# A matrix-memory attention layer between two routed FFNs: output steps moved by chunks, norm double-buffered, biases folded

## What is computed

```
xn = LN(x) * g + b ;  x_t = xn W_up_l + b ;  r_t = xn W_up_r + b
x_c = silu(causal_conv(x_t))                    # conv along features
q, k = x_c W_q + b, (x_c W_k + b) / 8 ;  v = x_t W_v + b ;  o = sigmoid(x_t W_o + b)
i, f = 15 tanh((x_c W + b) / 15)                # per head
m_t = max(f + m, i); c = exp(f - m_t + m) c + exp(i - m_t) v k^T ; n likewise
h   = o * (c q) / max(n q, 1)                   # 8 heads of 64, scan over 512 tokens
hn  = LN_head(h) * mh_g + mh_b
out = (hn + x_c W_skip + b) * silu(r_t) ; result = out W_down + b + x
```

## Time and profile before

| | us |
|---|---|
| runs of the kernel before (3) | 540.03, 540.77, 541.8; median 540.77 |
| profiled execution, whole | 539.02 |
| its span | 537.2 |
| mean granted TensorE clock | 0.885 |
| ffn(0) up to the last block | about 107 |
| attention, its head included | about 107 to 440 |
| ffn(1) | to 537 |

### The profile page before, as it was taken

The page is one execution under the profiler, slowest core; times in us unless marked ns, Lnnn a source line. Parts: engine busy times, 40 slices in busy tenths (PEclk is TensorE's granted clock), DMA queues, the critical chain, the costliest instruction groups (busy, mean ns, idle before and its releaser), DMA issues.

```text
span 537.2 us, 9897 instructions
## 1 busy us (share of the span) xinstructions
PE 392.7 (73%) x3018; PEld 329.4 (61%) x3035; DVE 343.2 (64%) x988; ACT 207.7 (39%) x528; POOL 194.9 (36%) x172
## 2 busy tenths in 40 slices
PE   0851499907998799897999988898998632049990
PEld 0720499904786677675777766676776522049990
DVE  5677277777259787379684497892889425027763
ACT  0230144435444474544635355634554100014440
POOL 5248244430005542224353054223062532724451
PEclk9996599957999999999979998999998755559996
DMA  8999222120000000000000000000004000112215
GB/s 299 296 327 209 54 66 69 59 88 2 0 1 1 2 2 1 1 0 0 0 0 0 0 0 0 0 0 0 1 1 157 2 0 10 49 46 69 68 56 166
DMA packets 26394, 28.23 MB, mean 53 GB/s; under 512 B 2977, under 2 KB 23329, under 8 KB 25857
## 3 DMA queue, kind: packets, MB, share of 16 engines
q1 hardware_dynamic: 22144, 19.13, 13.6%
q0 software_dynamic: 2496, 5.13, 2.9%
q10 hardware_dynamic: 1728, 3.65, 1.9%
HBM read 18.69 MB, written 9.21 MB: 52 GB/s over the span
## 4 chain that ended last, share of the span: by engine, by line
PE 50%; DVE 18%; POOL 9%; DMA 8%; issue 8%; ACT 5%; DVEq 0%; SPq 0%; ACTq 0%; POOLq 0%
PE bank L760 45%; POOL slots L467 6%; DMA slots<-QKT 3%; PE bank L1028 1%; DVE X L1149 1%; DMA X<-x 1%; PE bank L938 1%; DVE XN L1167 1%; PE bank L827 1%; DMA QKT<-by_token 1%; DVE CS L1512 1%; DMA by_token<-YB,IDX 1%; ACT WVT L656 1%; ACT E L665 1%; DMA slots<-XN,POS 1%
## 5 line engine op out<-in xcount | busy, mean ns | idle before, releaser
L493 POOL TENSOR_TENSOR HS<-HS,MHALF 128x8 f32<-128x8 f32 x16 | 26.3, 1644 | 202.6 <-DVE HS L1544 202.6
L473 POOL DMA_INDIRECT by_token<-YB,IDX x46 | 44.5, 968 | 60.1 <-DVE YB L1254 59.5
L760 PE MATMUL bank<-XBT,W1R 128*128 128x128 f32 x368 | 52.8, 290 | 0.0
L656 ACT ACTIVATE WVT<-bank,AC 128x128 f32<-128x128 f32 x128 | 36.5, 374 | 36.5 <-PE bank L760 36.5
L760 PE MATMUL bank<-W,HT 128*128 x368 | 49.2, 278 | 0.0
L467 POOL DMA_INDIRECT slots<-XN,POS x32 | 35.3, 1102 | 38.4 <-DMA slots<-QKT 17.2
L760 PEld LDWEIGHTS bank<-XBT,W1R 128*128 128x128 f32 x368 | 48.0, 204 | 0.6 <-ACT XBT L562 0.2
L827 PE MATMUL bank<-K,XB 128*128 128x128 f32 x46 | 13.6, 296 | 46.0 <-DMA XB<-slots 45.8
L760 PEld LDWEIGHTS bank<-W,HT 128*128 128x128 f32 x368 | 45.5, 195 | 0.3
L562 ACT ACTIVATE XBT<-bank 128x128 f32<-128x128 f32 x46 | 12.8, 277 | 84.5 <-PE bank L827 84.5
L620 ACT ACTIVATE QKT<-bank,COLS 128x512 f32<-128x512 f32 x32 | 22.0, 687 | 38.8 <-PE bank L760 38.8
(11 more groups left out here) (281 smaller groups left out, 1039.7 us busy)
## 6 DMA issues: line engine op xcount, KB each, us to landing
W<-w SPq DMA_DIRECT2D x2, 2048.0 KB, 13.4
slots<-QKT SPq DMA_DIRECT2D x2, 1483.5 KB, 25.3
XB<-slots SPq DMA_DIRECT2D x46, 64.5 KB
W<-w SPq DMA_DIRECT2D x1, 2064.0 KB, 22.9
QKT<-by_token SPq DMA_DIRECT2D x8, 256.0 KB, 4.2
X<-x SPq DMA_DIRECT2D x4, 256.0 KB, 4.9
BROWS<-rowpack SPq DMA_DIRECT2D x1, 1024.0 KB, 12.6
out<-X SPq DMA_DIRECT2D x4, 256.0 KB, 2.3
```

The costliest lines, as they stand in the source:

```text
L473: g.indirect_dma_start(out=by_token[f], out_offset=bass.IndirectOffsetOnAxis(ap=IDX[:, j:j + 1], axis=0), in_=YB[:, j, :], in_offset=None) ...
L493: step.do(g.tensor_tensor(HS[:, 3, :], HS[:, 2, :], MHALF[:, 0:H], ALU.pow))
L656: ins = a.activation(DT[:, hf, m, :], DM[:, m * P:(m + 1) * P], ACT.Exp, bias=AC[:, c, h:h + 1])
L760: return t_.matmul(o, l, r, start=start, stop=stop, skip_group_check=True)
```

## The change

Six things are done.

- VectorE: `centre` is cut into `divide` and `centre`; both for chunk `c` now stand in chunk `c + 1`, with `weigh` between them. `gate` and `transpose_out` of chunk `c` come in chunk `c + 2`, the transpose behind its `values`; `norm_moments` moves from chunk 1 to chunk 0, `silu` and `gate_scans` inside chunk 3.
- The transpose bank's order follows (`TR_USES`).
- `H2` has two buffers, `H2S[c % 2]`; the second lies over `YB`.
- The norm's g and b and the biases of v, o and r are folded into the weights at the start, through a column of ones in place of feature 0 of `ZB`; the v, o and r projections have no bias matmul, the s projection has one of an fp32r row pair. `XT` and one load (`WUL`) go.
- These weights are split during the setup, no longer behind the last block.
- On ScalarE, `out_t` and the head's copies change places accordingly.

```diff
-        TR_USES = ["k0", "k1", "u0", "k2", "u1", "o0", "d0", "k3", "u2", "o1", "d1", "o2", "d2", "o3", "d3"]
+        TR_USES = ["k0", "k1", "u0", "k2", "u1", "k3", "u2", "o0", "d0", "o1", "d1", "o2", "d2", "o3", "d3"]
...
-        H2 = w1r_flat[:, 0:HID].rearrange("p (h d) -> p h d", h=H)
+        H2S = [w1r_flat[:, 0:HID].rearrange("p (h d) -> p h d", h=H),
+               YB[:, :, :].rearrange("p j d -> p (j d)").rearrange("p (h d) -> p h d", h=H)]
...
             def head_in(b):
 
                 act.wait_ge(*pj_full_at(b, "z"))
-                a.activation(XT[:, :], PJ[0][:, :], ACT.Identity, scale=col("g"), bias=col("b"))
-                a.activation(XTH[:, :], PJ[0][:, :], ACT.Identity, scale=col("g"), bias=col("b"))\
-                 .then_inc(pj_free[0], 1)
+                a.activation(XTH[:, :], PJ[0][:, :], ACT.Copy).then_inc(xt_high, 1)
...
                 if c:
                     decays(b, c, 0)
-                if c >= 2:
-                    out_t(b, c - 2)
+                if c == 3:
+                    out_t(b, 0)
                 if last and c == 3:
                     xn_channels(1, 0)
                 if nxt:
                     take(*nxt, "v")
+                if c == 3 and not last:
+                    round_xc(b + 1)
                 decays(b, c, 1)
                 if c:
                     squares(b, c - 1)
...
                     xn_channels(1, 1)
                 if nxt:
                     take(*nxt, "o")
+                if c == 3 and not last:
+                    head_gates(b + 1)
                 state_decays(b, c)
-                if c == NC - 1 and not last:
-                    round_xc(b + 1)
-                    head_gates(b + 1)
                 if nxt:
                     take(*nxt, "r")
                 if c < NC - 1:
...
             def sequence(b, last):
                 for c in range(NC):
                     chunk(b, c, last)
-                if not last:
-                    for m in range(3):
-                        head_qk(b + 1, m)
+                if last:
+                    out_t(b, 1)
+                    squares(b, 3)
+                    out_t(b, 2)
+                    out_t(b, 3)
+                    return
+                head_qk(b + 1, 0)
+                out_t(b, 1)
+                head_qk(b + 1, 1)
                 squares(b, 3)
-                if not last:
-                    head_qk(b + 1, 3)
+                head_qk(b + 1, 2)
+                head_qk(b + 1, 3)
                 out_t(b, 2)
-                if not last:
-                    for m in range(4, 8):
-                        head_qk(b + 1, m)
-                    take(b + 1, 0, "s")
-                    head_columns(b + 1)
-                    decays(b + 1, 0, 0)
+                for m in range(4, 8):
+                    head_qk(b + 1, m)
+                take(b + 1, 0, "s")
+                head_columns(b + 1)
+                decays(b + 1, 0, 0)
                 out_t(b, 3)
...
                 dst = pj_wait(b, f"{what}{c}")
-                mm(dst[:, :], ONES3[:, :], BIAS3[:, i * HID:(i + 1) * HID], True, False)
-                for x_, w_ in parts:
-                    ins = mm3(dst[:, :], x_, w_, False, x_ is parts[-1][0])
+                if what == "s":
+                    mm(dst[:, :], ONESR[:, :], SKIPB[:, :], True, False)
+                for n, (x_, w_) in enumerate(parts):
+                    ins = mm3(dst[:, :], x_, w_, what != "s" and n == 0, n == len(parts) - 1)
...
-                if c >= 2:
-                    transpose_out(b, c - 2)
                 if last and c == 3:
 
                     xn_channels(1, 0)
                 if nxt:
                     project(*nxt, "v")
                 decays(b, c, 1)
-                if c >= 2:
-                    down_out(b, c - 2)
+                if c == 3:
+                    down_out(b, 0)
                 if nxt:
                     project(*nxt, "o")
                 if last and c == 3:
...
                 from_state(b, c)
                 if more:
                     to_state(b, c)
+                if c == 2 and not last:
+                    head_x(b + 1)
                 values(b, c)
+                if c >= 2:
+                    transpose_out(b, c - 2)
                 if last and c == 3:
                     for q in range(3):
                         logits(1, q)
-                if c == 2 and not last:
-                    head_x(b + 1)
 
             def open_sequence(b):
 
...
                 for c in range(NC):
                     chunk(b, c, last)
                 if last:
+                    down_out(b, 1)
                     for c in (2, 3):
                         transpose_out(b, c)
                         down_out(b, c)
                     return
-                head_qk(b + 1, WQH, WQL, "q", lambda: head_carry(b + 1))
+
+                def after_first():
+                    down_out(b, 1)
+                    head_carry(b + 1)
+
+                head_qk(b + 1, WQH, WQL, "q", after_first)
                 transpose_out(b, 2)
                 head_qk(b + 1, WKH, WKL, "k", lambda: down_out(b, 2))
                 project(b + 1, 0, "s")
...
             def low_xt(b):
-                dve.wait_ge(*pj_read_at(b, "z"))
-                v.tensor_tensor(XTL[:, :], XT[:, :], XTH[:, :].bitcast(F32), ALU.subtract).then_inc(xt_low, 1)
+                dve.wait_ge(xt_high, b + 1)
+                v.tensor_tensor(XTL[:, :], PJ[0][:, :], XTH[:, :].bitcast(F32), ALU.subtract).then_inc(pj_free[0], 1)
...
-            def centre(b, c):
+            def divide(b, c):
...
                 dve.wait_ge(hv_read, n + 2)
+            def centre(b, c):
+
+                H2 = H2S[c % 2]
                 dve.wait_ge(*pj_read_at(b, f"o{c}"))
...
             def chunk(b, c, last):
                 more = c < NC - 1
                 if c:
+                    divide(b, c - 1)
                     weigh(b, c, 0)
+                    if c == 3 and not last:
+                        silu(b + 1)
+                    centre(b, c - 1)
+                    if c == 3:
+                        update_x(b, 0)
                 else:
                     take_k(b, 0)
-                if c >= 2:
-                    update_x(b, c - 2)
-                if c:
-                    variance(b, c - 1)
                 if more:
                     take_k(b, c + 1)
                 weigh(b, c, 1)
                 scale_q(b, c)
-                if c == 3 and not last:
-                    low_xc(b + 1)
-                    gate_scans(b + 1)
-                    take_r(b + 1, 0)
                 if more:
                     take_r(b, c + 1)
+                elif not last:
+                    low_xc(b + 1)
+                if c:
+                    variance(b, c - 1)
+                if c == 0 and not last:
+                    norm_moments(b + 1)
+                if c == 1 and not last:
+                    scale_norm(b + 1)
+                if c == 2 and not last:
+                    low_xt(b + 1)
+                if c >= 2:
+                    gate(b, c - 2)
                 if last and c == 0:
                     layer_moments(1, 0)
                 if last and c == 2:
                     layer_norm(1, 0)
-                if c == 1 and not last:
-                    norm_moments(b + 1)
                 if more:
                     new_state(b, c)
-                if c == 2 and not last:
-                    low_xt(b + 1)
-                if c:
-                    gate(b, c - 1)
-                if c == 1 and not last:
-                    scale_norm(b + 1)
-                centre(b, c)
-                if c == 2 and not last:
-                    silu(b + 1)
+                elif not last:
+                    gate_scans(b + 1)
+                    take_r(b + 1, 0)
 
             def sequence(b, last):
                 for c in range(NC):
                     chunk(b, c, last)
+                divide(b, 3)
+                centre(b, 3)
+                gate(b, 2)
                 if not last:
                     reset_state()
+                variance(b, 3)
+                update_x(b, 1)
+                if not last:
                     gate_rows(b + 1)
-                variance(b, 3)
                 update_x(b, 2)
                 gate(b, 3)
                 if not last:
...
-                for i, (low, weights, high) in enumerate(((WVL, WVF, WVH), (WOL, WOF, WOH), (WURL, WURT, WURH))):
-                    dve.wait_ge(w_high, i + 1)
```

139 lines of the change are left out of this document (75 added, 64 removed).

## The result

| | before | changed |
|---|---|---|
| median of the runs beside each other, us | 540.4 (539.53 to 541.8) | 551.16 (548.78 to 555.36) |
| ratio, 95% interval | | 1.0199 (1.0169 to 1.023) |
| span of the profiled execution | 537.2 | 550.0 |
| mean granted clock in it | 0.885 | 0.855 |

The change made the kernel slower by 2%; measured again later (run 16) it took 545.56 us, 1.0089 (1.0064 to 1.0115) of the kernel before. The forecast was 535.1 us, and both figures lie above its range of 529.5 to 542.

The account below looks back on a forecast made before the run. TensorE plus its waits was taken to set the pace; -5.4 us over three looped sequences and -0.3 for a load gave -5.7, from a median of 540.77 to 535.1 us, range 529.5 to 542.

Parts of the forecast that it names:

- The walk: One looped sequence walked in program order with full-clock durations: 71.8 us instead of 73.6, 1.8 us less.
- r': Chunk 3: TensorE's r projection of the next sequence waits 1.1 us, with take(o) behind squares on ScalarE.
- The wait of 0.5 ahead of the state decays: Chunk 3: silu ahead of centre(2) delays it by 1.1 us, so the state decays wait 0.5 us.
- Norm_moments and centre: VectorE: norm_moments in chunk 0 takes 2.7 us instead of 4.6; centre(1) beside GpSimd takes 1.3 more, ending at 26.6.
- I keep these 3.4 us in the forecast.: Clock loss of the kernel before, 2.3 and 1.1 us in its second and third sequences, assumed unchanged.
- Rival C: Looped sequences: half clock in every one, 14.7 us lost instead of 3.4, 546 us; decided by 5.7 extra; chance 0.13.
- with 8 us of waits, lost nothing: Argument against half clock everywhere: the first sequence of the kernel before had 8 us of waits and kept full clock.
- Together 0: Last sequence: 2.1 us of biases gone, state product 1 us later, 0.8 back; net 0, ends -2 and +2.
- The fold's 2.8 us: Looped sequences: twelve v, o and r bias matmuls of 0.23 us removed, 2.8 us less a sequence.
- 1.0 as new waits: Looped sequence: new TensorE waits of 9.0 us against old ones of 8.0, so 1.0 us more.
- The forecast's -0.3: Opening: one load of 128 KB less ahead of the slot fill, -0.3 us; weight splits in the setup cost 0.
- Rival B: Looped sequences: smaller waits or steadier clock; 531.4 us without clock loss, 531 if centre(1) is not stretched; chance 0.20.

Follow-up runs that it names:

- run 16: The changed kernel itself measured once more, unedited: 545.56 us, 1.0089 (1.0064 to 1.0115) of the kernel before.
- run 9: The changed kernel with mask matmuls filling TensorE's waits only ahead of s(2) and s(3), those of chunk 3 left open: 544.17 us.
- run 10: The changed kernel with mask matmuls only in chunk 3, ahead of the next sequence's r and the last state product: 533.79 us.
- run 7: The changed kernel with one mask matmul put ahead of each v, o and r projection, where the bias matmul stood before: 536.26 us.
- run 4: The changed kernel with new state (2) computed ahead of the twelve layer norms in the last sequence: 542.68 us.
- run 18: The kernel of run 1 with new state (2) ahead of the layer norms in the last sequence: 530.49 us.
- run 11: Run 1 plus run 3, with the twelve layer norms, their transposes and router matmuls moved out of the last sequence's chunks 2 and 3: 527.34 us.
- run 14: The kernel of run 12 with one mask matmul put ahead of each v, o and r projection: 523.4 us.
- run 6: The kernel before, in its old order, without the bias matmuls of its v, o and r projections: 537.37 us.
- run 5: The kernel before with mask matmuls in its waits for OUT, X and QS, four of them in a bank ScalarE had yet to read: 543.59 us.
- run 3: The changed kernel with ScalarE's OUTT copy for chunk 1 ahead of its conversion of q(0): 536.38 us.
- run 17: The kernel of run 4 measured again, beside the changed kernel on one chip: 543.94 us.
- run 2: The changed kernel with four OT buffers instead of two and ScalarE's copy of o ahead of the squares: 547.75 us.
- run 15: The kernel of run 12 without its 8 + 7 mask matmuls a looped sequence: 532.38 us.
- run 1: The changed kernel with 17 mask matmuls a looped sequence where TensorE waited for the OT copy and QS: 531.71 us.
- run 8: Run 1 plus run 3, with new states first in the last sequence and six layer norms behind that of chunk 1, six behind chunk 2's: 532.27 us.
- run 12: The kernel of run 11 with four OT buffers, and 8 mask matmuls ahead of head_z and 7 ahead of state product (3) instead of 17: 522.23 us.

## Why the prediction was wrong

**The walk was right in its sum.** At full clock a looped sequence takes 71.5 us (forecast 71.8), 2.1 under the 73.6 of before. The waits against it: s(2) 0.66 (0.9), s(3) 1.85 (2.3), head_z 0.48 (0.8), r' 0.88 (1.1), QS 1.32 (1.6), down_out(1) 1.26 (1.4). The wait of 0.5 ahead of the state decays did not show.

**Norm_moments and centre.** VectorE's timeline in chunk 0: without GpSimd beside it the tiny operation took 0.17 us, as forecast:

```profile
156.15 0.17 DVE L1158 TENSOR_SCALAR LA<-LA 128x4 f32<-128x4 f32 x1
```

Of centre(1), beside head_norm(0) and add_bdown, the reduce kept its time, the subtraction did not (VectorE's timeline), and GpSimd's operation took 1.75 us where it takes 1.26:

```profile
172.91 0.69 DVE L1560 TENSOR_REDUCE HS<-YB 128x8 f32<-128x512 f32 x1
174.09 1.72 DVE L1562 TENSOR_TENSOR YB<-YB,HS 128x512 f32<-128x512 f32 x1
```

The row of GpSimd's timeline:

```profile
172.28 1.75 POOL L502 TENSOR_TENSOR W1R<-W1R,HT 128x512 f32<-128x512 f32 x1 [0.17 <-POOL W1R L499]
```

Centre(1) ended at 26.9 us, forecast 26.6. The Trainium skill, "SBUF — State Buffer" (section "Who interferes with whom"), says that tensor_reduce never contends with GpSimd; the 0.69 us beside GpSimd agrees.

**The step that failed: "I keep these 3.4 us in the forecast."** The clock term was 16.6 us in the three looped sequences, 13.2 more than I kept. Rival C was this: its mechanism, its point of decision (5.7 us of extra loss) and nearly its price, 14.7 us for three sequences, which lost 5.8, 2.5 and 8.3. Its 546 us and the 6 of the last sequence make 552. I gave it 0.13. That the price came near is partly luck: 4.9 us a sequence was read from the half clock of a sequence that was only 2.3 us longer. My argument against it, that the first sequence of before "with 8 us of waits, lost nothing", counted waits by their sum; runs 9 and 10 show that their place counts. It was also one sequence of three with the same code, and the other two had lost clock.
The Trainium skill, "TensorE: Matmul & The Clock Gate" (section "A second HAM failure mode: psum-queue depth-cycling"), says that brief idling between groups of matmuls can make the clock swing. By that rule the change should have been suspected; the runs agree, 16.6 us by the windows, but in run 7 much the same idling left the clock alone.

**The step "Together 0" for the last sequence** failed by 6.1 us, outside its own ends of -2 and +2. VectorE came to the twelve layer norms 1.4 us later in its sequence (411.53 - 379.97 = 31.6 us, before 30.2): QS came as early as before (29.0 us in both), but variance(1) and gate(0), which used to be done ahead of it, now stand between take_r(3) and them. TensorE reached its wait for the state 1.9 us earlier. Then TensorE's timeline shows:

```profile
418.54 1.09 PE L1041 MATMUL bank<-K,OUT 128*128 128x128 f32 x4 [5.12 <-DVE CS L1533]
428.25 1.77 PE L768 MATMUL bank<-CS,QS 64*128 64x65 f32 x16 [2.86 <-DVE QS L1525]
429.95 3.67 PE L768 MATMUL bank<-VX,WOT 128*128 128x65 f32 x16
434.27 5.12 PE L768 MATMUL bank<-WR,XNT 128*128 128x8 f32 x24
```

The wait had grown from 1.90 to 5.12 us, state product (3) came at 48.3 us instead of 44.3 (the walk had it 1 us later), and values and router matmuls ran at half clock: 3.67 and 5.12 us, before 2.00 and 2.80. Of the 6.1 us, 4.0 lie ahead of the state product and 2.1 behind. For runs 4 and 18 I took the wait for the cause; run 18 shows that VectorE's queue, with the layer norms in it, is: only moving them out (run 11) brought 3 us.

**The fold's 2.8 us.** The sum booked them as a gain and 1.0 as new waits. Run 7 and run 14 give the fold 0.2 us a sequence in the new order (0.7 in the old, run 6); it was the order that saved 1.9. The total was right and its split was not: TensorE's busy time is no bound where VectorE's chain sets the ends, which the earlier trace rows, with its waits for VectorE, could have told.

**The opening.** The forecast's -0.3 came out as -0.16, but that is one profile. Over sixteen profiles with the changed opening it took 145.5 to 149.0 us, 147.3 on average; over four with the old one 148.5 to 149.8, on average 149.3. So it is likely some 2 us shorter, and why stays open.

**A slip.** Rival B without any clock loss is 535.1 - 3.4 = 531.7 us, not 531.4; nothing hangs on it.

## What to carry to other kernels

Where TensorE waits for others, taking work off it does not shorten the chain but lengthens its idleness, and the granted clock can fall behind it: look at clock and waits stretch by stretch. Neither the longest wait nor their sum told here where it would fall: mostly behind three waits of 0.9 to 1.3 us close together, but also behind single ones of 1.8 and 2.1 us, and in run 7 behind neither. To tell a clock loss from a longer chain, put matmuls into a free bank, of the waits' size, in place of the waits: if the kernel gets faster with more work, it was the clock. A filler must write a bank that is already free, or it is a wait of its own (1.77 us in run 5).

## What the runs showed that was not expected

- Kernels with open waits spread more: 12 to 14 us in runs 3, 4, 5, 9 and 17, of seven to ten executions each. Of four executions each, the change, runs 2 and 15 spread by 6 to 7 us and run 16 by 2.6, and those whose waits of chunk 3 were filled (1, 8, 10, 11, 12, 18) by 0.8 to 3.5. The Trainium skill, "TensorE: Matmul & The Clock Gate" (section "What's actually happening"), says that the number of matmuls that a kernel runs at the low clock at its start differs from run to run. No run here counts those; the spreads here go with waits inside the kernel.
- Taking away a wait of 1.26 us, three times, was worth 9 to 15 us (run 3). In the profiled execution the half clock behind the waits ahead of it was much shorter.
- Twelve layer norms of 128x128 took 6.06 us in the change and 6.10 in run 18, and 5.47 before.
